# Gated delta stage: TensorE's and ScalarE's work dealt anew to a pass's four gaps, and every stage's weights loaded in the layernorm ahead of it

## The reference, cut to what matters

```
x = layernorm(x + L0_attn(x))     # gated delta rule, 16 heads of 64 x 64 state
x = layernorm(x + L0_ffn(x))      # ternary feed-forward
x = layernorm(x + L1_attn(x))     # disentangled attention (relative positions)
x = layernorm(x + L1_ffn(x))      # hashed mixture of experts
x = layernorm(x + L2_attn(x))     # RWKV-6 recurrence
x = layernorm(x + L2_ffn(x))      # low-rank linear
x = layernorm(x + L3_attn(x))     # rotary attention
x = layernorm(x + L3_ffn(x))      # routed mixture of experts
```

```
q, k, v = silu(causal_conv4(x @ W.T) + bias)      # k is also scaled by 1/8
a    = sigmoid(x @ Wa.T + ba);  beta = sigmoid(x @ Wb.T + bb)
def step(S, (qt, kt, vt, at, bt)):                # S: 64 x 64 per head and sequence
    err = S @ kt - vt
    S   = at[:, None] * S - bt * outer(err, kt)
    return S, S @ qt
o = ((o - mean) / sqrt(var + eps) * ln_w + ln_b) * sigmoid(x @ Wg.T)
out = o @ Wo.T
```

## Time and profile before

| | |
|---|---|
| median of three runs | 3490.7 us |
| profiled execution, its own time | 3488.99 us |
| its span | 3487.2 us |
| TensorE busy | 2785.7 us (80%) |
| VectorE busy | 2254.9 us (65%) |
| ScalarE busy | 1308.9 us (38%) |
| GpSimd busy | 375.5 us (11%) |
| mean granted TensorE clock | 0.851 of full speed |
| gated delta stage and its layernorm | 0 to 1510.6 us |

### The profile page before, as it was taken

The page is one execution under the profiler, slowest core; times in us unless marked ns, Lnnn a source line. Parts: engine busy times, 40 slices in busy tenths (PEclk is TensorE's granted clock), DMA queues, the critical chain, the costliest instruction groups (busy, mean ns, idle before and its releaser), DMA issues. The chain is left out here.

```text
span 3487.2 us, 65560 instructions
## 1 busy us (share of the span) xinstructions
PE 2785.7 (80%) x25436; PEld 1817.2 (52%) x25488; DVE 2254.9 (65%) x3961; ACT 1308.9 (38%) x2809; POOL 375.5 (11%) x348
## 2 busy tenths in 40 slices
PE   5777777777777777869569999986675677789998
PEld 5777676777676667723246666642222122234443
DVE  4989888888888988811347777824564666332222
ACT  2233333333333333332357777741113355422223
POOL 0000000000000000000210110002232111044443
PEclk8787777777877877789779999997787799889999
DMA  4111111111111111020189999700000111121110
GB/s 151 26 27 26 26 26 26 26 26 26 26 26 26 26 26 26 2 57 0 29 223 247 232 231 248 184 17 31 0 0 22 55 41 41 43 82 30 30 33 30
DMA packets 194794, 213.99 MB, mean 61 GB/s; under 512 B 29842, under 2 KB 175650, under 8 KB 189138
## 3 DMA queue, kind: packets, MB, share of 16 engines
q1 hardware_dynamic: 194529, 210.03, 22.9%
HBM read 142.71 MB, written 67.03 MB: 60 GB/s over the span
## 5 line engine op out<-in xcount | busy, mean ns | idle before, releaser
L577 DVE SCALAR_TENSOR_TENSOR rf_A<-ps,rf_bias,rf_G 128x512 f32<-128x512 f32 x152 | 114.1, 751 | 274.6 <-POOL rf_G L559 260.1
L2052 PE MATMUL ps<-dl_kqN,dl_ST 64*64 64x32 f32 x4224 | 205.7, 271 | 32.2 <-DVE dl_ST L2390 27.8
L2367 DVE TENSOR_REDUCE dl_ZO<-dl_XP 128x64 f32<-128x128 f32 (+6 forms) x448 | 219.6, 490 | 15.4
L1111 DVE TENSOR_REDUCE ra_top<-ps 128x1 f32<-128x512 f32 x256 | 161.5, 684 | 96.0 <-PE ps L915 89.4
L2052 PEld LDWEIGHTS ps<-dl_kqN,dl_ST 64*64 64x64 f32 x4224 | 201.6, 198 | 37.3 <-issue 36.8
L559 POOL TENSOR_TENSOR rf_G<-rf_G,rf_WB 128x512 f32<-128x512 f32 x144 | 182.2, 1265 | 280.7 <-ACT rf_G L548 280.7
L548 ACT ACTIVATE rf_G<-ps,rf_bias 128x512 f32<-128x512 f32 x152 | 104.4, 687 | 287.2 <-PE ps L529 287.2
L2363 DVE TENSOR_TENSOR dl_XP<-dl_ZO,dl_G 128x64 f32<-128x64 f32 (+6 forms) x448 | 194.6, 434 | 15.4
L1309 POOL MEMSET da_K<- 32x4096 f32 x2 | 7.2, 3576 | 1707.8 <-POOLq L82 1707.8
L1768 DVE TENSOR_REDUCE da_top<-ps 128x1 f32<-128x512 f32 x256 | 177.0, 692 | 8.8
L1619 ACT ACTIVATE da_E<-ps,da_top 128x512 f32<-128x512 f32 x256 | 176.1, 688 | 17.4 <-DVE da_top L1768 17.0
(11 more groups left out here) (352 smaller groups left out, 6129.9 us busy)
## 6 DMA issues: line engine op xcount, KB each, us to landing
da_bands<-da_AB SPq DMA_DIRECT2D x128, 384.0 KB, 3.8
dl_Abc<-dl_ends SPq DMA_DIRECT2D x64, 512.0 KB, 6.1
da_window<-da_bands SPq DMA_DIRECT2D x128, 192.0 KB, 4.4
da_across<-da_bands SPq DMA_DIRECT2D x128, 192.0 KB, 4.5
rf_WB<-rf_shares SPq DMA_DIRECT2D x48, 256.0 KB, 3.2
da_parts<-da_split SPq DMA_DIRECT2D x64, 96.0 KB, 3.3
rf_We<-in_rf_We SPq DMA_DIRECT2D x1, 4608.0 KB, 15.8
da_K<-da_parts SPq DMA_DIRECT2D x16, 256.0 KB
```

What stands on the lines that cost most here:

```text
L1111: eng.tensor_reduce(top[:, m % 2, u:u + 1], ps[:, score_bank(UNITS * m + u), :], AXX, ALU.max, negate=True).then_inc(s["maxima"], 1)
L2052: mm = eng.matmul(start_ps[rows, pair, :], ST[rows, pair, :], kqN[rows, pair, e * CH:(e + 1) * CH, :].rearrange("p t k -> p (t k)"), start ...
L2367: link(eng.tensor_reduce(ZO[:, to:to + 1 + (2 * I - 1) * CH:CH].rearrange("p (k i) -> p k i", k=2), XP[:, :, :, SB - 1 - t:], AXX, ALU.add))
```

## The change

It has two parts.

**The gated delta stage.** (1) `later_products` writes accumulator banks 4 and 5 and no longer 6 and 7. TensorE runs it within `boundary(n, 1)`, behind the state update and ahead of the next start, after VectorE has read the keys' products; before, it ran ahead of `boundary`. ScalarE's copy of it moves behind the copies of `boundary(n, 1)`, and the state update's wait for that copy goes. (2) The first group of the keys' projection moves from ahead of `boundary(n, 0)` to behind it, with its evacuation. (3) ScalarE makes the copy of `middle(n, 0)` ahead of the evacuation of the A groups and not behind it. (4) The scaled copies of the keys become a function of their own, called behind the copy of `middle(n, 1)`. (5) The product with Wo reads its operand with one step of 8 numbers over 128 elements, where it read 4 runs of 32 elements with a step of 32.

**The stages' weights.** Each stage becomes a generator that hands its list of loads to the layernorm ahead of it, whose SyncE list issues them. `layernorm` also asks for the table of the natural logarithm at the start of ScalarE's list.

```diff
-def layernorm(c):
+def layernorm(c, loads):
...
+        @block.sync
+        def _(eng):
+            for sem, pairs in loads:
+                load_all(eng, sem, pairs)
...
         @block.scalar
         def _(eng):
+            eng.preload_act_table_set("natural_log")
...
+        yield [(loaded, pairs)]
         block = c.block(ctx)
         @block.sync
         def _(eng):
-            load_all(eng, loaded, pairs)
...
-        later_ps = ps[:, 6:8, :].rearrange("p h (a n x) -> p h a n x", n=GR, x=XC // 2)
+        later_ps = ps[:, 4:6, :].rearrange("p h (a n x) -> p h a n x", n=GR, x=XC // 2)
...
                 def next_start(r):
                     eng.wait_ge(s["state"], j4 + r + 1)
-                    if e == 1 and r == 0:
-                        eng.wait_ge(s["gt"], 2 * n + 4)
...
                 eng.wait_ge(s["wc"], 6 * n + 3 * e + 3)
-                if e == 1:
-                    eng.wait_ge(s["ktc"], 5 * n + 6)
...
+                if e == 1:
+                    eng.wait_ge(s["gt"], 2 * n + 3)
+                    eng.sem_inc(c.past, 1)
+                    later_products(n + 1)
                 for r in range(GR):
                     next_start(r)
...
-                Dv = D[:, :].rearrange("p (t b m) -> p m b t", m=M, b=B)
+                Dv = D[:, :].rearrange("p (t m) -> p m t", m=M)
...
-                project(n + 1, 2, 5, False)
-                eng.wait_ge(s["evac"], (n + 1) * PROJ + 5)
+                project(n + 1, 2, AV, False)
+                eng.wait_ge(s["evac"], (n + 1) * PROJ + AV)
...
                 boundary(n, 0)
-                project(n + 1, 5, 6, True)
+                project(n + 1, AV, 6, True)
...
                     eng.wait_ge(s["wo_copied"], n)
-                eng.sem_inc(c.past, 1)
-                later_products(n + 1)
                 boundary(n, 1)
...
                 eng.wait_ge(s["prep"], 2 * n + 2)
+                middle(n, 0)
                 evacuate(n + 1, 0, 2)
-                middle(n, 0)
                 if not first:
                     deviation(n - 1)
-                evacuate(n + 1, 2, 5)
+                evacuate(n + 1, 2, AV)
                 boundary(n, 0)
-                evacuate(n + 1, 5, 6)
+                evacuate(n + 1, AV, 6)
                 if not first:
                     out(n - 1)
                 middle(n, 1)
+                scaled_keys(n + 1)
                 evacuate(n + 1, 6, PROJ)
+                boundary(n, 1)
                 later_products(n + 1)
-                boundary(n, 1)
...
-        for layer in LAYERS:
-            layer(c)
-            layernorm(c)
+        stage = LAYERS[0](c)
+        next(stage)
+        for layer in LAYERS[1:]:
+            for _ in stage:
+                pass
+            stage = layer(c)
+            layernorm(c, next(stage))
+        for _ in stage:
+            pass
+        layernorm(c, [])
         store_end(c)
```

More of the change, by code:

```diff
@@ L1217, in relative_attention @@
         heads = c.sb("da_heads", [P, HEADS], ctx)
+        PT = c.sb("da_PT", [P, 2, QUAD, T], ctx)
+        early = PT[:, :, :, :].rearrange("p s h t -> p (s h t)")
+        rel = early[:, 0:256].rearrange("p (k x) -> p k x", k=2)
+        Wp = early[:, 256:512].rearrange("p (k x) -> p k x", k=2)
+        pairs = [(Wp, d["da_Wp"]), (rel, d["da_rel"]), (bias[:, :], d["da_bias"]), (W[:, :, :], d["da_W"]), (heads[:, :], d["da_heads"]),
+                 (bv[:, :], d["da_bv"]), (bo[:, :], d["da_bo"]), (place[:, :, :], d["da_place"])]
+        yield [(s["loaded"], pairs)]
         ends = c.sb("da_ends", [P, 1], ctx)
@@ L2109, in out @@
                 eng.sem_inc(c.past, 1)
-                Dv = D[:, :].rearrange("p (t b m) -> p m b t", m=M, b=B)
+                Dv = D[:, :].rearrange("p (t m) -> p m t", m=M)
                 for m in range(M):
-                    mm = eng.matmul(ps[:, 6, 0:P], Wo[:, m, :], Dv[:, m, :, :], start=m == 0, stop=m == M - 1)
+                    mm = eng.matmul(ps[:, 6, 0:P], Wo[:, m, :], Dv[:, m, :], start=m == 0, stop=m == M - 1)
                 mm.then_inc(s["wo"], 1)
@@ L2154, in _ @@
             products_of_keys(0)
-            later_products(0)
             eng.wait_ge(s["gt"], 2)
             eng.sem_inc(c.past, 1)
+            later_products(0)
             for r in range(GR):
@@ L2162, in _ @@
                 one_pass(n, False)
+            eng.wait_ge(s["ktc"], 5 * NC + 1)
             centre(NC - 1)
@@ L2185, in evacuate, with scaled_keys @@
                     ins.then_inc(s["evac"], 1)
-                    if w == K and half == 1:
-                        eng.wait_ge(s["evac"], m * PROJ + i + 1)
-                        for e in range(2):
-                            span = slice(e * CH, (e + 1) * CH)
-                            eng.activation(kqN[:, :, span, 0], kc[:, e, :, :], ACT.Copy, scale=scale)
-                            ins = eng.activation(kkN[:, :, :, span], kc[:, e, :, :].unsqueeze(2).to_broadcast([P, NP, 2, CH]), ACT.Copy, scale=scale)
-                        ins.then_inc(s["kq"], 1)
+            def scaled_keys(m):
+                eng.wait_ge(s["evac"], m * PROJ + 6)
+                for e in range(2):
+                    span = slice(e * CH, (e + 1) * CH)
+                    eng.activation(kqN[:, :, span, 0], kc[:, e, :, :], ACT.Copy, scale=scale)
+                    ins = eng.activation(kkN[:, :, :, span], kc[:, e, :, :].unsqueeze(2).to_broadcast([P, NP, 2, CH]), ACT.Copy, scale=scale)
+                ins.then_inc(s["kq"], 1)
             def later_products(m):
@@ L2227, in out @@
                 eng.wait_ge(s["wo"], n + 1)
-                eng.activation(back, ps[:, 6, 0:P].rearrange("p (b t) -> p b t", b=B), ACT.Copy).then_inc(s["wo_copied"], 1)
+                eng.activation(back, ps[:, 6, 0:P].rearrange("p (t b) -> p b t", b=B), ACT.Copy).then_inc(s["wo_copied"], 1)
             def middle(n, e):
@@ L2261, in _ @@
             eng.activation(beta[:, 0:T], ps[:, 7, :], ACT.Sigmoid, bias=vec[:, BB:BB + 1]).then_inc(s["beta"], 1)
-            evacuate(0, 0, PROJ)
+            evacuate(0, 0, 6)
+            scaled_keys(0)
+            evacuate(0, 6, PROJ)
             eng.wait_ge(s["staged_q"], 32 + 16 * len(late))
```

27 lines of the change are left out of this document (6 added, 21 removed).

## The result

The changed kernel took 3349.4 us (median of 4 runs, 3344.7 to 3351.3); the kernel before, on the same chip, 3491.2 us (3490.6 to 3493.7). The ratio is 0.9593, 95% interval 0.9579 to 0.9607: 142 us less. The forecast was 3379 us with a range from 3348 to 3430, so the measured time lies 1.4 us above the range's lower end. The profiled span fell from 3487.2 to 3346.3 us.

What follows compares the result with a forecast made beforehand. VectorE, fullest in the gated delta stage, waits 112.3 us for TensorE there; seams and layernorms are serial. Gains of 67 + 8 + 37 = 112 us from 3489.0 leave 3377, plus 1.7 gives 3379 us, range 3348 to 3430.

Steps and rivals of the forecast that it cites:

- rival 4: Gated delta stage: TensorE stays at the upper clock level because its idle time is filled, starts run faster: 3337 us, 8%.
- Update waits: Gated delta stage: of VectorE's 57.9 us of waits for the state update all but 3 go, 55 us gained.
- Gap after the first half: 16 passes: without the K group TensorE's transposes begin 3.3 us earlier, when W is there, so the update wait goes.
- The price of the moved K group: Second half's middle: 3.7 us of work into 3.08 idle, 0.2 us late a pass, set to 0; ends 0 and 59 lost.
- Cross products: Head of a pass: ScalarE's copy to WT goes about 1.8 us earlier; 22 of 30.1 us gained, ends 14 and 30.
- `later_products`, 10 us lost: End of a pass: 64 matmuls between update and start cost 0.6 us in all 16 passes; ends 3 and 22.
- the prediction's own signs of being wrong: Cross-product waits in the second half's middle, starts at the upper level, Wo product 1.9 us, lower granted clock, late loads.
- Rivals 1 to 3: 1: TensorE's clock stays low, 3546 us, 3%; 2: late by half that, 3427, 15%; 3: waits migrate, 3446, 8%.
- Layernorms, 8 us: Eight layernorms: with the table already loaded the last Ln ends 1.0 us earlier in each; ends 5 and 10.
- Seams, 37 us: Between stages: first work no longer waits for weights, which load inside the layernorm ahead; 36.9 us gained, ends 30 and 42.
- The Wo product: Gated delta stage: reading with a step of 8 is as slow as 32, so no gain, still near 3.7 us.

Runs made afterwards that it cites:

- the kernel with the seams alone: The kernel before with only the early weight loads and the table load at the layernorm's start, gated delta stage as before: 3442.7 us, ratio 0.9863.

## Why the prediction was right, and where it was not

The direction and most terms held, but that the time lay inside the range is partly luck. It came 30 us under the forecast and 7 us under the forecast's own best of 3356; only the stretch toward rival 4 let the range reach down to 3348. In the profiled runs the miss is 29 us: 6 in the seams, 10 in the term for `later_products`, 4 in the cross products, 1 in the update waits, 3 in two smaller waits that had no term, and 4 in no view of waits. Point by point:

- **Update waits, 55 us.** Measured 55.9. But the reason given for it was only one of two, and this is the step that failed: "Gap after the first half" takes the K group as the cause of the wait. It is a cause: moved alone, edit (2) ends it. It is not the one that the changed kernel needs. Edit (3), which the step does not name, lets TensorE begin the cross products earlier and at the upper level: with it they start 0.78 us after the transposes. Variance and V groups follow at the upper level too (1.98 us for the variance instead of 3.78 in the kernel with edit (2) alone). That head start holds the 3.73 us of a K group, and with it the group cost nothing where it stood.
- **The price of the moved K group, 0.** The step looked for it in the gap where the group lands and rightly found none there: no wait at L2328 in the second half's middle. Its reason was wrong, though. It held that lateness there counts in full; the transposes began up to 1.4 us after VectorE's W (0.8 in the pass shown), and VectorE did not wait. The price is in the gap it left: 3.75 us of idle time, a granted clock of 0.50 behind it, and starts that come late. It is 12.8 us, by the run that undoes edit (2). Of rival 4's rule the prediction noted only the good side, idle time filled; the change also opens a hole.
- **Cross products, 22 us.** Measured 26.4 in the trace, and 26 us by the run that undoes edit (3). Inside the bounds (14 to 30). Its worth on its own was missed: 69 us over the kernel with the seams alone, since it also ends the update wait of the first half and shortens what follows.
- **`later_products`, 10 us lost.** Mis-sized: some 2 us at the end of a pass, and nothing in the sum. VectorE waited for the start at the end of a pass 9 times, 8.6 us in all, before, and 6 times, 10.1 us, after; the sum over all starts stayed at 24. The step took the start behind `later_products` to be waited for in every pass; it ran in 3.92 us, at the upper level, in 10 of 16, and in these VectorE did not wait. The whole of edit (1), its share of the update waits included, is worth 9 us by the run that undoes it.
- **Rival 4** (starts at the upper level, 3337) came half true: at the end of most passes, not after the first half. Starts at the upper level were also one of the prediction's own signs of being wrong, and this sign came. With edit (2) undone it came nearer, and the time was 3336.6. That this is the rival's 3337 proves little, since the starts after the first half there still took about 5 to 6 us, and not 3.92.
- **Rivals 1 to 3** did not come. The two K groups took 9.32 us, where 7.5 would be the upper level's and 14.9 the lower's. With the Wo product behind them they were done at 703.5, 1 us after VectorE's W, and that lateness cost no wait.
- **Layernorms, 8 us.** Measured 8.3, with luck in it: 0.97 in each of five, and 4.0, 0.1 and -0.7 in the other three. In those three the mean's products ran at different levels before and after (6.74 us against 3.67, 5.69 against 6.57, 3.67 against 5.31). Eight times 0.97 would be 7.8.
- **Seams, 37 us.** Measured 43.2. The step took a block change of TensorE at 1.2 us; behind a layernorm it is ready 0.3 us after X, idle 5.5 us in all instead of 7.4. Of these 1.9 us, 1.0 is the layernorm's own gain, which has a term of its own, and 0.9 the mis-sized block change. Low-rank, forecast at 2.4, was right by luck: 3.3 us of idle time went beyond the layernorm's share, and its product L360 took 6.76 us where it had taken 5.86. In the RWKV stage 14.9 us came for 11.8: the first product started 11.5 us sooner after X, and the products behind it ran faster (L646, the old L650, 4.14 us against 4.96). In the rotary stage 3.4 came for 1.6, and which part of it is the clock is not shown. In the ternary stage the 10.7 held within 0.2 us.
- **The Wo product** did not gain, as said. It lost 0.2 us, which was not.

For the second half's update wait, about 26 us in the kernel with the seams alone, the runs give this: edit (2) alone ends it, edits (1), (4) and (5) together end it, edit (3) alone does not (26.5 us stay). What stays open: some 4 us of the stage that no wait shows; what edit (4) does, which was not tried alone; and why the granted clock after the first half followed more than the idle time right ahead of it.

## What to carry to other kernels

A wait between two engines can have several sufficient cures, so a part of a change is measured by undoing it from the whole and by adding it alone to the old, and the two numbers may differ in sign: the K group's move was worth 41 us alone and cost 13 us on top of the rest. Before work is taken out of an engine's gap because something behind it is late, look for what delays the gap's beginning: one ScalarE copy moved ahead of eight others did more than any moved matmul. Built up from the seams alone, edits (3), (2) and the group (1), (4), (5) gave 69, 41 and 44 us; all five together gave 93. And time in which TensorE idles ahead of a chain of small matmuls may not be free: here 3.75 us of it came with a chain at the lower level. It has to be read in the trace, since moving the idle time from one place of the gap to another gained nothing.

## What the runs showed of the chip

- A start of 128 recorded matmuls (64 x 32) takes 7.04 us at a granted clock of 0.50 and 3.92 at 1.00; 5.18 us at 0.78 lie between.
- Reading TensorE's moving operand with a step of 8 in one run of 128 elements took 3.89 us for 16 matmuls, with a step of 32 in four runs of 32 elements 3.69.
- From the last write of X to the next stage's first matmul TensorE needed about 0.3 us in the hashed, low-rank and routed stages, less than the 0.95 us for which it sat idle between the stage's last work and the layernorm's first product.
- Removing a table load of 1.28 us between two activations of ScalarE made a layernorm 1.42 us shorter (12.30 to 10.88), and removing eight gave 10.2 us.
- Moving one line of ScalarE's order raised TensorE's mean granted clock too: from 68 to 1400 us it was 0.78 in the kernel with the seams alone and 0.81 with that line moved. How much of the 69 us came through the clock and how much through the waits themselves is not shown.
